# Attention beside routed experts on one core: scatters, gathers, a DMA queue's order and the expert steps set at other places in a fixed schedule

## What is computed

```python
x = L0_attn_x                                    # (1, 2048, 128)
xn = _layernorm(x)
# attention: 16 heads of 64
q, k, v = (xn @ Wq), (xn @ Wk), (xn @ Wv)        # each (1, 2048, 16, 64)
scores = jnp.einsum('bqhd,bkhd->bhqk', q, k) * SCALE
out = einsum('bhqk,bkhd->bqhd', softmax(scores), v) @ Wo + bo
# experts: the one with the largest logit
expert_ids = argmax(softmax(xn @ router_w.T))    # of 8
h = square(relu(xn @ expert_fc[e]))              # 128 -> 512
ffn = h @ expert_proj[e].T                       # 512 -> 128
return x + out + ffn
```

## Time and profile before

| what | value |
| --- | --- |
| time, median of 3 runs | 1406.76 us (1405.45 to 1407.57) |
| the profiled execution: time, span | 1407.44 us, 1405.7 us |
| granted TensorE clock, mean | 0.993 |
| PE busy (matmuls) | 1372.5 us, 98% |
| POOL busy | 1127.5 us, 80% |
| DVE busy | 1076.7 us, 77% |
| ACT busy | 737.6 us, 52% |

### The profile page before, as it was taken

One profiled execution on the slowest core, in us unless ns is written; L12 is line 12 of the kernel. 1 busy time (PEld: TensorE's weight loads), 2 busy tenths in 40 slices (PEclk: granted clock), 3 DMA queues, 4 the chain that ended last, 5 costly groups with the idle time before them and its releaser, 6 DMA issues.

```text
span 1405.7 us, 20002 instructions
## 1 busy us (share of the span) xinstructions
PE 1372.5 (98%) x6447; PEld 865.1 (62%) x6447; DVE 1076.7 (77%) x1465; ACT 737.6 (52%) x1318; POOL 1127.5 (80%) x911
## 2 busy tenths in 40 slices
PE   6899999999999999999999999999999999999998
PEld 4555665656756666656666566666576565666554
DVE  6898877767777677777777776787777777787897
ACT  5354654645645546546456455455464464565453
POOL 6798877878877778777788778787787787889996
PEclk9999999999999999999999999999999999999999
DMA  3422112321123111222113220132111231110100
GB/s 83 112 66 63 40 25 63 85 51 42 30 59 91 44 42 42 66 72 54 32 42 72 67 66 19 43 92 68 45 34 41 73 72 23 24 27 10 33 24 15
DMA packets 65095, 72.12 MB, mean 51 GB/s; under 512 B 8992, under 2 KB 38240, under 8 KB 64992
## 3 DMA queue, kind: packets, MB, share of 16 engines
q1 hardware_dynamic: 63968, 68.75, 20.0%
q0 software_dynamic: 1024, 2.10, 0.5%
HBM read 17.83 MB, written 5.11 MB: 16 GB/s over the span
## 4 chain that ended last, share of the span: by engine, by line
PE 86%; DVE 6%; DMA 2%; SPq 2%; ACT 1%; issue 1%; POOL 1%; POOLq 0%; DVEq 0%; ACTq 0%
PE OB L1100 30%; PE SB L1056 15%; PE SB L1060 14%; PE MB L1078 14%; PE XB L1137 2%; PE XB L1128 2%; PE XB L1146 2%; PE XB L1045 2%; DVE mx L762 2%; SPq L365 2%; DVE low L898 1%; PE XB L1038 1%; POOL acc L495 1%; ACT high L629 1%; DMA Q<-mrow 1%
## 5 line engine op out<-in xcount | busy, mean ns | idle before, releaser
L495 POOL TENSOR_TENSOR acc<-acc,ex 128x512 f32<-128x512 f32 x720 | 922.2, 1305 | 101.6 <-ACT ex L609 39.2
L762 DVE TENSOR_REDUCE mx<-MB 128x1 f32<-128x512 f32 x992 | 659.2, 687 | 248.6 <-PE MB L1078 244.9
L609 ACT ACTIVATE ex<-SB 128x512 f32<-128x512 f32 x1024 | 607.0, 598 | 348.4 <-PE SB L1060 288.4
L1100 PE MATMUL OB<-ex,V 128*64 128x512 f32 x2048 | 452.6, 594 | 0.0
L1056 PE MATMUL SB<-Q,K 128*128 128x512 f32 x1024 | 423.1, 413 | 0.2 <-ACT ex L609 0.2
L1060 PE MATMUL SB<-Q,K 128*128 128x512 f32 x1024 | 401.5, 392 | 5.7 <-DMA Q<-mrow 5.7
L1078 PE MATMUL MB<-K,Q 128*128 128x512 f32 x992 | 389.5, 394 | 2.8 <-DVE mx L762 2.1
L1100 PEld LDWEIGHTS OB<-ex,V 128*64 128x64 f32 x2048 | 143.8, 137 | 284.5 <-issue 273.0
L1056 PEld LDWEIGHTS SB<-Q,K 128*128 128x128 f32 x1024 | 194.0, 189 | 92.2 <-issue 53.5
L1060 PEld LDWEIGHTS SB<-Q,K 128*128 128x128 f32 x1024 | 193.7, 189 | 40.7 <-DMA Q<-mrow 8.9
L1078 PEld LDWEIGHTS MB<-K,Q 128*128 128x128 f32 x992 | 187.0, 189 | 47.7 <-DVE mx L762 6.9
(11 more groups left out here) (142 smaller groups left out, 610.9 us busy)
## 6 DMA issues: line engine op xcount, KB each, us to landing
Q<-high SPq DMA_DIRECT2D x124, 128.0 KB, 2.3
K<-high SPq DMA_DIRECT2D x112, 128.0 KB, 2.3
Q<-low SPq DMA_DIRECT2D x64, 128.0 KB, 2.3
K<-low SPq DMA_DIRECT2D x56, 128.0 KB, 2.3
w<-fc SPq DMA_DIRECT2D x23, 256.0 KB, 2.7
w<-projT SPq DMA_DIRECT2D x23, 256.0 KB, 3.1
sorted_x<-res SPq DMA_DIRECT2D x1, 1472.0 KB, 6.8
tok<-sorted_x SPq DMA_DIRECT2D x23, 64.0 KB, 1.7
```

Source lines behind the costliest of these rows:

```text
L495: pool.tensor_tensor(a[:, :], src[:, :], EX[h][ex_slot(kt)][:, :], ALU.add).then_inc(done, 1)
L609: act.activation(EX[h][ex_slot(kt)][:, :], SB[bank_of(n, 2 * kt + h)][:, :], ACT.Exp).then_inc(a_e[h], 1)
L762: dve.tensor_reduce(mx[:, m % 2, u:u + 1], MB[bank_of(m, i)][:, :], AX.X, ALU.max).then_inc(v_m, 1)
L1100: mm = pe.matmul(OB[own[h], :], V[(n // JB) % 2][:, k, own[h]], EX[h][ex_slot(k)][:, :], start=(k == 0), stop=(k == NT - 1))
```

## The change

Six things are set differently; no arithmetic is changed.

- Scatters: before in blocks 0 (`kt` 10 to 15) and 1 (`kt` 1 to 10), now eight each in blocks 1 and 2 at `kt` 2, 4, 6, 10 to 14. `find_slots` moves from block 0 to `kt` 0 of block 1, `find_owners` from block 1 to block 3, `d_sort` becomes two semaphores, and VectorE takes one addition more in block 2.
- Tiles: blocks 4 to 26 in place of 3 to 25.
- Expert steps: transpose, up and down at key tiles 3, 4 and 11 in place of 2, 3 and 10.
- SyncE's queue: the maxima go ahead of Wo and of the tile's store. The filling with zeros goes from the start into block 0, behind the maxima of block 1.
- Fetches: in blocks 28 and 29 at `kt` 10 to 14 and in block 30 at 10 to 15, in place of 2, 4, 6, 8, 11, 14 and of 1, 3, 5, 7.
- Results added: one part each at `kt` 2 to 5 of block 31, in place of two each at 14 and 15 of block 30.

```diff
-AT_TOK, AT_UP, AT_DOWN = 2, 3, 10
+AT_TOK, AT_UP, AT_DOWN = 3, 4, 11
 TILES = NT + E - 1
-TILE0 = 3
+TILE0 = 4
 AT_RANK = 7
-AT_PLACE, AT_OWN = 8, (1, 0)
-SORT = [(0, kt) for kt in range(10, NT)] + [(1, kt) for kt in range(1, 11)]
-FETCH = [(n, kt) for n in (NB - 4, NB - 3) for kt in (2, 4, 6, 8, 11, 14)] + [(NB - 2, kt) for kt in range(1, 8, 2)]
-BACK = {14: (0, 1), 15: (2, 3)}
+AT_PLACE, AT_OWN = {(0, 8): (0, 1), (1, 0): (2,)}, (3, 0)
+SORT = [(n, kt) for n in (1, 2) for kt in (2, 4, 6, 10, 11, 12, 13, 14)]
+FETCH = [(n, kt) for n in (NB - 4, NB - 3) for kt in range(10, 15)] + [(NB - 2, kt) for kt in range(10, NT)]
+BACK = {2: 0, 3: 1, 4: 2, 5: 3}
...
             if k == 1:
                 return {8: [4, 5, 6], NT: [12, 13, 14, 15]}
...
+            if k == 2:
+                return {8: [4, 5, 6], NT: [13, 14, 15]}
...
-                    sp.dma_start(sorted_x.rearrange("(r p) d -> p r d", p=P), under(res[:, :], TILES)).then_inc(d_res, 16)
                     place_max(Lin(0))
...
+                    if before(n, NB - 1):
+                        place_max(n + 1)
                     if n % JB == 1 and before(n, NB - JB):
                         load_wo(pair + 1)
+                    if n.off == 0:
+                        sp.dma_start(sorted_x.rearrange("(r p) d -> p r d", p=P), under(res[:, :], TILES)).then_inc(d_res, 16)
                     if has_tile(n):
                         store_tile(n - TILE0)
-                    if before(n, NB - 1):
-                        place_max(n + 1)
                     if n.off == TILE0 - 1:
-                        sp.wait_ge(d_sort, 16 * NT)
+                        for half in range(2):
+                            sp.wait_ge(d_sort[half], 16 * NT // 2)
...
-                            wait(act, d_sort, 16 * NT)
+                            wait(act, d_sort[c // 2], 16 * NT // 2)
...
-                        if start and kt == AT_PLACE:
-                            for part in range(3):
-                                rank(part)
+                        for part in AT_PLACE.get((n.off, kt), ()):
+                            rank(part)
                         if (n.off, kt) == AT_OWN:
                             find_owners()
-                        if n.off == NB - 2:
-                            for j in BACK.get(kt, ()):
-                                take_back(j)
+                        if n.off == NB - 1 and kt in BACK:
+                            take_back(BACK[kt])
```

More of the change, by code:

```diff
@@ L189, in layer @@
         a_q0 = sem("a_q0")
-        t_lg, t_rk, v_r, v_mask, v_slot, v_own, d_sort = (
-            sem(n_) for n_ in ("t_lg", "t_rk", "v_r", "v_mask", "v_slot", "v_own", "d_sort"))
+        t_lg, t_rk, v_r, v_mask, v_slot, v_own = (
+            sem(n_) for n_ in ("t_lg", "t_rk", "v_r", "v_mask", "v_slot", "v_own"))
+        d_sort = [sem(f"d_sort{k}") for k in range(2)]
         d_tile, t_tok, t_up, t_down, a_tok, a_up, a_res, g_hid, d_res, d_back, v_back = (
@@ L239, in on_dve @@
                 return {8: [5, 6], 12: [9, 10, 11, 12], 13: [13], 14: [14], NT: [15]}
-            if k == 0:
-                return {NT: [12, 13, 14, 15]}
             if k == 1:
                 return {8: [4, 5, 6], NT: [12, 13, 14, 15]}
-            return {8: [5, 6], NT: [12, 13, 14, 15] if k >= FETCH[0][0] else [13, 14, 15]}
+            if k == 2:
+                return {8: [4, 5, 6], NT: [13, 14, 15]}
+            return {8: [5, 6], NT: [12, 13, 14, 15] if k == 0 or k >= FETCH[0][0] else [13, 14, 15]}
         def on_pool(n, kt):
@@ L524, in sort_tokens @@
                     for k in ks:
-                        pool.indirect_dma_start(sorted_x, indexed(k), xn[:, k, :], None).then_inc(d_sort, 16)
+                        pool.indirect_dma_start(sorted_x, indexed(k), xn[:, k, :], None).then_inc(d_sort[2 * k // NT], 16)
                 def fetch_results(ks):
```

## The result

The changed kernel takes 1390.76 us (median of 4 runs, 1387.76 to 1392.0) against 1406.48 us of the kernel before, run beside it (median of 4, 1405.45 to 1407.57). The ratio is 0.9885, with a 95% interval of 0.9867 to 0.9903: 1.15% faster. I had said 1387, with a range of 1382 to 1395.

What follows compares the result with a forecast made beforehand. TensorE's own work bounds normal blocks, so only its waits and slow clock can yield time. Gains of 23.6 us less 3.6 lost gave 20.0: from 1407.4 to 1387 us, own range 1384 to 1390, with neighbours 1382 to 1395.

Steps and rivals of the forecast that it cites:

- (c): Blocks 6, 10, 14, 18, 22, 26: start without waiting for maxima queued behind Wo; 0.73 us each, 4.4 gained.
- (d): Twelve blocks with K parts and tiles: transpose and down product stop waiting for VectorE's `low`; 0.60 us each, 7.2 gained.
- (e): Blocks 28 and 29: projections no longer late once fetches leave the path to `normalise`; 2.7 us gained.
- the last block: Block 31: VectorE idles before its first addition, delaying the final chain; 3.0 us lost, from 0 to 6.5.
- (a): Block 0: maxima arrive earlier without the zero filling ahead, 2.0 us gained; fewer waits in its rest, 0.5.
- (b): Block 1: waits for VectorE's owners and ahead of the projection, and lost clock, go; 6.8 us gained.
- Blocks 2 and 3: Late scatters make ScalarE wait and the owners' step loads block 3; 0.6 us lost, from 0 to 2.
- a sign of being wrong: Blocks 2 and 3: ScalarE waiting for the scatters would count against the forecast; 0.5 us thought possible with bad luck.
- The term by the port lock: Block 3: owners' step as slow as in block 1 because GpSimd shares VectorE's port; 0.6 to 2 us.
- the rival of waits that take the place of those removed: Expert steps: waits move to other neighbours in XB or another reader; 1387 + 7 = 1394 us, chance 0.13.
- The bound for the end: Block 31: range of the loss from VectorE's idle time and a late last fetch, 0 to 6.5 us.

Runs made afterwards that it cites:

- old scatters: Changed kernel with scatters, find_slots, find_owners, zero filling and the division of additions in blocks 0 and 2 as before: 1400.69 us.
- owners in 1: Changed kernel with find_owners back in block 1, behind find_slots: 1389.95 us, ratio 0.9874 to the kernel before.
- steps back: Changed kernel with transpose, up and down product back at key tiles 2, 3 and 10: 1396.68 us, ratio 0.9929 to the kernel before.
- the old end: Changed kernel with fetches and additions of results at their places before the change: 1387.06 us, ratio 0.9865 to the kernel before.

## Why the prediction was right, and where not

The sum was 20.0 us, the profile gives 15.4, and the ratio gives 16.2 us. The sign and the range held, and so did the mechanism of terms (c), (d) and (e) and of the last block. In (a) and (b) half of the mechanism was wrong. The size of (b) was safe all the same, as it came from the comparison of block 1 with block 2; that the wait of (a) shrank as said is in part luck. Four terms were mis-sized.

- **Start and rest of block 0**, term (a): 2.5 said, 1.4 measured (0.6 lost ahead of block 0, 2.0 won in it). The wait shrank by 1.94 us as said, but I took for certain that the filling delays the maxima. It does where they follow it after 2.5 us (2.2 us lost) and not where 5.2 us lie between; the changed kernel with the filling back in its old place waits 1.22 us, no longer than without. The clock decides more here than the filling: it moves the start by up to 4.1 us, and block 0 is 35.64 to 35.67 long in the three profiles with full clock there, and 36.94 to 37.14 in the four with 6.3 to 6.8 us of half clock in it. The measured runs of the changed kernel spread over 4 us and those of before over 2, which fits that but doesn't prove it.
- **Block 1**, term (b): 6.8 said, 6.4 measured in the profile, 6.6 in the experiment with the old scatters. But the owners, whom I had given 1.75 us of it, have no price of their own: with the old scatters and owners that held up nobody, TensorE stood for 3.78 us at the projection alone, against 3.64 in two waits, and the block was as long. The scatters ahead of the projection and the half clock behind them make the loss. What is left is ScalarE's wait for the K copies; with the queries later it is gone and the block takes 40.39.
- **Blocks 2 and 3**: 0.6 lost said, 0.3 measured. ScalarE's wait for the scatters, which I had named as a sign of being wrong, came in block 3 (1.38 us) and is the price. The other half of the reason was wrong: the owners cost nothing in block 3, though their last instruction took 1.56 us there. The term by the port lock of the Trainium skill, "SBUF — State Buffer", section "SBUF: two separate sides", was 0.6 to 2; the lock may have lengthened the instruction, but nobody waited for it.
- **Maxima ahead of Wo**, term (c): 4.4 said; 0.68 in five blocks and about 0.75 in block 26 are 4.1, and the reversed edit gives 0.76 a block. The estimate of 0.73 lay between the two.
- **Expert steps**, term (d): 7.2 said, 5.6 measured over the twelve blocks. The price of 0.60 a block was exact in ten. In blocks 9 and 12 it was given back, as the queries' reader waits for K copies that a load of instructions makes late; the last section has the figures. With the queries a key tile later both blocks have the full gain. This pair of blocks is worth 1.6 us (2 x 0.60 + 0.42), and in these two the rival of waits that take the place of those removed came true, with a reader that I hadn't named.
- **Fetches**, term (e): 2.7 said, 2.7 measured. GpSimd was late after the scatters and fetches and recovered under the V batch, as said.
- **Last block**: 3.0 lost said, 4.2 measured, and 3.9 to 5.4 over the eight profiles with this end. The 3.4 us of idle were there, as 3.71, and 3.2 of them reach the end every time; what I had left out is that the final matmuls run at half the clock behind a longer idle, 1.0 us here and 0.6 to 2.2 over the profiles. The landing of the last fetch played no part: the first part of results starts without a wait.

The end (1.2), the expert steps (1.6) and the start (1.1) make 3.9 of the 4.6 us by which the sum was too large. The bound for the end reached to 6.5, so it was in the range; the late K copies were in no rival, and nothing in the rows I had chosen showed them, though 43.21 us of block 9 before against 42.79 of its kind would have.

The statement of the change has one thing to be added: VectorE also takes additions 5 and 6 of head 0 in block 0, by the last line of `on_dve`, so GpSimd's additions fall from 783 to 780. The 2.0 us won in block 0 hold that as well; it wasn't tried by itself.

## What to carry to other kernels

Work that is moved to fill an engine's idle time must be there when the gap is: a gap at a block's start can't take work that stands behind the first job of that block, and the late fetches cost more at the end than they won three blocks earlier, while the same fetches one block earlier won both. Compare blocks of one kind with each other before pricing an edit: one that is 0.4 us longer than its ten likes, like block 9 before, may have a neighbour that isn't in the program's order, and here the wait that was removed there came back behind another reader. And where the first tens of microseconds differ by 4 us between executions, judge an edit there by repeated runs, and one in the steady part by the profile.

## What the runs showed of the hardware

**An instruction of VectorE can be passed over for several of GpSimd's.** The same scan took 6.64 us with the old scatters, 0.42 in the kernel before and 1.25 in the changed kernel; GpSimd was adding meanwhile, one addition after the other. In all three the scan ended 0.28 or 0.29 us after the end of one of these additions: of the one that ran when the scan began in the two short cases, and of the sixth in the long one, behind which GpSimd paused. The last owners' instruction took 3.10 us beside a scatter and two additions, 1.56 beside a scatter and one, and 0.18 (owners in 1, old scatters) with nothing running on GpSimd. The Trainium skill, "SBUF — State Buffer", section "SBUF: two separate sides", states that the two engines share a port pair as an exclusive lock for the whole of one instruction, which whichever starts first gets, if VectorE's reads two inputs in SBUF or runs in a two-port mode. By that rule alone one would expect a wait of one addition of GpSimd at most, 1.3 us; 6.64 us go over five of them, so here the measurement decides: the wait can go over several. When this happens is not settled: the kernel before had 14 additions in a row at the same place and its scan was short. It could explain the two groups of runs with the old scatters, 1397 to 1398 and 1401 to 1406; only one of the long ones was profiled, so that is argued.

**Instruction loads lie among the data, and can make it late.** The DMA records of each profile hold 52 loads of instructions of 16 KB, which take 0.9 to 1.8 us of a DMA engine. In a K block the copies of the K part of key tile 1 have usually landed 17.6 us after the block's start. Eleven profiles have the queries at key tile 5, each with 12 such blocks. ScalarE waited for the copies in exactly those 22 of the 132 blocks in which a load began between 14.0 and 16.9 us after the block's start. These are blocks 9 and 12 in ten of the profiles, and 17 and 20 with the steps back, where the loads in 9 and 12 begin at 17.6 and 17.4, too late to matter. In block 12 of the changed kernel the last copy landed at 19.3 us. And the wait follows the load: in block 9, in the nine profiles with queries at 5 and steps at 3, 4 and 11, the load took 0.95 to 1.58 us and the wait was 0.20 to 0.25 us longer every time. With the queries at key tile 6 the loads still lie there (15.3 to 16.3 us) and nobody waits. No run moved a load by itself, and the shorter waits for K copies in blocks 0 and 1 (1.05 and 1.12 us in the changed kernel) have no load of this kind ahead of them; their cause is open.

**The clock at both ends.** With the same instructions up to there, TensorE ran at half its clock for 17.1 us around the start of block 0 in one profile (the changed kernel), for 6.8 in another (owners in 1) and not at all in a third (the old end), and the start took 43.2 to 47.3 us. At the end an idle of 3.1 to 3.5 us was followed in all nine such profiles by matmuls at half the clock (in the changed kernel 2.36 and 1.22 us); in the five with an idle of at most 0.6 the same matmuls ran at full clock (1.92 and 0.71).
